# Attention with a routed feed-forward layer on one core: the row maxima of the scores placed by 512 small transfers of single numbers, and another order of work at both ends

## The reference

```python
def _L0_attn_ref(x, w_q, w_k, w_v, w_o):          # x: (4, 1024, 128), 16 heads of 64
    scale = 1.0 / sqrt(64)
    q = einsum('bsd,hdk->bhsk', x, w_q); k = ...; v = ...
    scores = einsum('bhqk,bhmk->bhqm', q, k) * scale
    weights = softmax(scores, axis=-1)
    z = einsum('bhqm,bhmk->bhqk', weights, v)
    z = transpose(z, (0, 2, 1, 3)).reshape(b, s, h * dk)
    return x + einsum('bse,ed->bsd', z, w_o)

def _L0_ffn_ref(x, Wr, W1, W2):                   # 8 experts, 512 rows each at most
    probs = softmax(xf @ Wr); eidx = argmax(probs); p_tok = probs[eidx]
    rank = (number of earlier tokens with the same expert); keep = rank < cap
    xe = xf[dispatch]
    ye = relu(xe @ W1) @ W2 * p_tok               # token's own expert only
    return y.at[dispatch].add(ye)

x = L0_attn_x
x = x + _L0_attn_ref(_layernorm(x), ...)
x = x + _L0_ffn_ref(_layernorm(x), ...)
```

## Time and profile before

| | |
|---|---|
| median of 3 runs | 1506.01 us (1503.90 to 1507.67) |
| the profiled execution's own time | 1504.45 us |
| its span in the profile | 1502.5 us, so 1.95 us lie around it |
| PE, PE's loads | 98%, 56% of the span |
| DVE, ACT, POOL | 66%, 52%, 81% |
| granted TensorE clock, mean | 0.992 |
| DMA packets | 125293, 137.88 MB |

### The profile page before, as it was taken

One profiled execution on the slowest core, in us unless ns is written; L12 is line 12 of the kernel. 1 busy time (PEld: TensorE's weight loads), 2 busy tenths in 40 slices (PEclk: granted clock), 3 DMA queues, 4 the chain that ended last, 5 costly groups with the idle time before them and its releaser, 6 DMA issues.

```text
span 1502.5 us, 21668 instructions
## 1 busy us (share of the span) xinstructions
PE 1477.6 (98%) x7240; PEld 840.9 (56%) x7240; DVE 995.6 (66%) x1222; ACT 784.0 (52%) x1540; POOL 1217.7 (81%) x676
## 2 busy tenths in 40 slices
PE   8999999999999999999999999999999999999897
PEld 5455555555555555555555555555555655555586
DVE  6557666676767656666666666676667766777543
ACT  4465555555555555555555555565554555544331
POOL 5888779898798878988788878889789998899645
PEclk9999999999999999999999999999999999999899
DMA  6334444432444434333344443334444334340431
GB/s 146 84 86 98 92 114 101 115 93 59 93 100 93 115 83 94 86 79 84 86 107 101 97 94 78 85 86 93 95 96 101 89 72 102 92 107 23 133 84 34
DMA packets 125293, 137.88 MB, mean 92 GB/s; under 512 B 44106, under 2 KB 69197, under 8 KB 125184
## 3 DMA queue, kind: packets, MB, share of 16 engines
q1 hardware_dynamic: 118784, 130.26, 37.3%
q0 software_dynamic: 2048, 4.10, 0.9%
q10 hardware_dynamic: 4352, 2.13, 0.5%
HBM read 16.81 MB, written 8.45 MB: 17 GB/s over the span
## 4 chain that ended last, share of the span: by engine, by line
PE 88%; POOL 5%; DVE 3%; issue 1%; ACT 1%; SPq 1%; DMA 1%; POOLq 0%; ACTq 0%; DVEq 0%
PE ps_w L1391 27%; PE ps_w L1375 16%; PE ps_w L1376 14%; PE ps_m L1323 10%; POOL acc L662 4%; PE ps_m L1424 3%; PE ps_w L1409 2%; PE ps_m L1291 2%; PE ps_m L1292 2%; PE ps_m L1293 2%; PE ps_w L1698 1%; PE ps_m L1698 1%; PE ps_m L1308 1%; PE ps_m L1309 1%; PE ps_m L1310 1%
## 5 line engine op out<-in xcount | busy, mean ns | idle before, releaser
L662 POOL TENSOR_TENSOR acc<-acc,ring 128x1024 f32<-128x1024 f32 x383 | 920.8, 2404 | 50.3 <-ACT ring L831 2.3
L1063 DVE TENSOR_REDUCE mxw<-ps_m 128x1 f32<-128x1024 f32 x512 | 601.8, 1217 | 324.1 <-PE ps_m L1323 321.1
L831 ACT ACTIVATE ring<-ps_w 128x512 f32<-128x512 f32 x1024 | 544.3, 600 | 251.6 <-PE ps_w L1376 236.4
L1391 PE MATMUL ps_w<-ring,V 128*64 128x512 f32 x2048 | 467.7, 598 | 0.0
L1375 PE MATMUL ps_w<-queriesA,keysA 128*128 128x512 f32 x1024 | 431.6, 422 | 2.7 <-issue 1.4
L1376 PE MATMUL ps_w<-queriesB,keysB 65*128 65x512 f32 x1024 | 406.4, 397 | 0.0
L1391 PEld LDWEIGHTS ps_w<-ring,V 128*64 128x64 f32 x2048 | 135.7, 136 | 265.5 <-issue 236.1
L662 POOL TENSOR_TENSOR acc<-ring 128x1024 f32<-128x1024 f32 x64 | 152.2, 2377 | 158.9 <-PE ps_w L1409 150.6
L1375 PEld LDWEIGHTS ps_w<-queriesA,keysA 128*128 128x128 f32 x1024 | 193.6, 189 | 103.5 <-issue 48.7
L1376 PEld LDWEIGHTS ps_w<-queriesB,keysB 65*128 65x128 f32 x1024 | 194.4, 190 | 33.6 <-issue 0.7
L1323 PE MATMUL ps_m<-keysA,queriesA 64*128 64x512 f32 x1000 | 183.0, 444 | 0.9 <-DVE mxw L1063 0.6
(11 more groups left out here) (185 smaller groups left out, 985.5 us busy)
## 6 DMA issues: line engine op xcount, KB each, us to landing
queriesA<-qk_high SPq DMA_DIRECT2D x248, 128.0 KB, 2.4
keysB<-qk_high SPq DMA_DIRECT2D x124, 128.0 KB, 2.4
keysA<-qk_rest SPq DMA_DIRECT2D x124, 128.0 KB, 2.4
queriesB<-qk_rest SPq DMA_DIRECT2D x124, 128.0 KB, 2.4
by_sums<-sums SPq DMA_DIRECT2D x240, 64.0 KB, 2.0
keysA<-qk_high SPq DMA_DIRECT2D x93, 128.0 KB, 2.4
tokens_by_slot<-blank ACTq DMA_DIRECT2D x16, 130.0 KB, 3.2
ring<-tokens_by_slot SPq DMA_DIRECT2D x8, 260.0 KB, 5.3
```

The costliest lines, as they stand in the source:

```text
L662: pool.tensor_tensor(acc[h][:, :], before, P_both(kt), ALU.add).then_inc(summed, 1)
L831: act.activation(P_tile(kt, p), ps_s[k % 3][:, :], ACT.Exp, scale=SCALE).then_inc(exp_done, 1)
L1063: dve.tensor_reduce(mxw[h][:, p * HT + qt:p * HT + qt + 1], ps_m[p][:, :], AX_X, ALU.max).then_inc(maxed, 1)
L1391: mm = pe.matmul(ps_z[p * DK:(p + 1) * DK, :], V_of(j, kt, p), P_tile(kt, p), start=(kt == 0), stop=(kt == KT - 1))
```

## The change

Between column and row nothing is computed any more. `turn_max` and `copy_max`, the tiles `mxt` and the semaphores `c_turned` and `c_copied` are gone. `place_max` waits for the last maximum itself (`maxed`) and issues, for each of the two heads and each of the four query tiles, one transfer from a column of `mxw[h]` (128 partitions, one number of 4 B each) to 128 neighbouring numbers of the row: 8 issues in place of 2, 1024 single numbers in place of 8 rows of 512 B. DVE waits for `c_placed`, where it waited for `c_turned`, before it writes over `mxw[h]`. The rest is order at the ends: the first projections of values stand between the first visits, there are 21 turns of `spin` at the start where there were 16, `choose`, `add_totals` and `find_slots` stand ahead of `end_root`, the moments are a part of their own (`end_moments`), PE counts the ranks ahead of the last softmax sums, and ACT copies these sums ahead of `shares`.

```diff
-        mxw = [sb(f"mxw{i}", [P, 2 * HT]) for i in range(2)]
-        mxt = [sb(f"mxt{i}", [2 * HT, P], F32R) for i in range(2)]
+        mxw = [sb(f"mxw{i}", [P, 2 * HT], F32R) for i in range(2)]
...
             def place_max(j, par, h):
-                sp.wait_ge(c_copied, 2 * j + h + 1)
+
+                sp.wait_ge(maxed, 8 * (2 * j + h) + 8)
                 for p in range(2):
-                    sp.dma_start(queriesB[par][p][DK:KC, h * HALF:(h + 1) * HALF].bitcast(F32)
-                                 .rearrange("o (t q) -> o t q", q=P),
-                                 mxt[h][p * HT:(p + 1) * HT, :].bitcast(F32)).then_inc(c_placed, 16)
+                    for t in range(HT):
+                        at = h * HALF + t * P
+                        sp.dma_start(queriesB[par][p][DK:KC, at:at + P].bitcast(F32),
+                                     mxw[h][:, p * HT + t:p * HT + t + 1].bitcast(F32)).then_inc(c_placed, 16)
...
-            def copy_max(j, h, bank):
-                act.wait_ge(c_turned, 2 * j + h + 1)
-                act.activation(mxt[h][:, :], bank[0:2 * HT, 0:P], ACT.Copy).then_inc(c_copied, 1)
...
             copy_z(LAST, 1)
+            copy_sums_out(LAST, 1)
             shares(B - 1)
-            copy_sums_out(LAST, 1)
...
-                            dve.wait_ge(c_turned, 2 * j + (1 if oct == 1 else 2))
+                            dve.wait_ge(c_placed, 128 * (2 * j + (1 if oct == 1 else 2)))
...
             in_order(dve, pair)
+            choose(B - 1, lent_out)
+            add_totals(B - 1)
+            find_slots(B - 1, lent_out)
             end_root(0)
             end_root_done(0)
-            choose(B - 1, lent_out)
             shift(B - 1)
-            add_totals(B - 1)
-            find_slots(B - 1, lent_out)
+            end_half(1)
             find_shares(B - 1)
-            end_half(1)
+            end_moments(1)
...
-            def turn_max(j, h, bank):
-                pe.wait_ge(maxed, 8 * (2 * j + h) + 8)
-                pe.transpose(bank[0:2 * HT, 0:P], mxw[h][:, :], ident[:, :]).then_inc(c_turned, 1)
...
                 if k == 0 and oct % 2 == 0:
-                    pe.wait_ge(c_placed, 32 * (2 * j + h) + 32)
+                    pe.wait_ge(c_placed, 128 * (2 * j + h) + 128)
...
-            spin(16)
+            spin(21)
...
             first_visit(0, 0)
+            pe.wait_ge(first_copied, 1)
+            project_v(0, 0, 0, 0, ps_s[0])
             first_visit(1, 1)
             first_visit(1, 0)
-            pe.wait_ge(first_copied, 1)
-            project_v(0, 0, 0, 0, ps_s[0])
+            pe.wait_ge(first_copied, 2)
+            project_v(0, 0, 1, 0, ps_s[1])
             first_visit(2, 1)
             first_visit(2, 0)
-            pe.wait_ge(first_copied, 2)
-            project_v(0, 0, 1, 0, ps_s[1])
+            pe.wait_ge(first_copied, 3)
+            project_qk(1, 1, 0, 0)
...
+            count_ranks(B - 1, lent_out)
             softmax_sums(LAST, 1, LAST_BY_PE)
-            count_ranks(B - 1, lent_out)
```

More of the change, by code:

```diff
@@ L860, in pair @@
                         cast_qk(1, 1, 2)
-                    if oct == 1:
-                        copy_max(j, 1, lent_max)
-                    if oct == 3 and not last:
-                        copy_max(j + 1, 0, lent_max)
                     if early(j, 0) is not None and oct >= 2:
@@ L1106, in end_half, with end_moments @@
                                                  op0=ALU.mult, op1=ALU.add).then_inc(end_added, 1)
+            def end_moments(h):
+                n, b = 2 * B - 1, B - 1
                 for t in range(h * HT, (h + 1) * HT):
@@ L1557, in pair @@
                         count_ranks(routed(j, "d"), lent_turn)
-                    if oct == 1:
-                        turn_max(j, 1, lent_max)
-                    if not last and oct == 3:
-                        turn_max(j + 1, 0, lent_max)
                     for k in range(5, 8):
@@ L1589, in pair @@
                             pe.wait_ge(ranks_read, routed(j, "d") + 1)
-                        if oct in (1, 3):
-                            pe.wait_ge(c_copied, 2 * j + 2 + oct // 2)
                         if oct == 1:
```

7 lines of the change are left out of this document (1 added, 6 removed).

## The result

| | before | after |
|---|---|---|
| median (4 runs each) | 1504.95 us (1502.17 to 1507.67) | 1692.47 us (1681.08 to 1703.92) |
| ratio to before, 95% interval | | 1.1247 [1.1207, 1.1288] |
| the profiled execution's own time | 1504.45 us | 1691.89 us |
| its span; mean granted clock | 1502.5 us; 0.992 | 1689.9 us; 0.939 |

What follows compares the result with a forecast made beforehand. PE, busy for 98% of the span, was taken to bound the kernel. 1504.45 - 7 (transposition) + 90 (waits) + 48 (clock) - 1 - 1.5 (ends) = 1633 us, range 1550 to 1690 us.

Steps and rivals of the forecast that it cites:

- Eight issues, second half: SP's issues of the second half's maxima, 0.64 us each, make PE wait 2.8 us at oct 2: 32 waits, 90 us.
- The 32nd wait: The very first placement, ahead of pair 0's first scores, counted as one more PE wait of 2.8 us.
- Single numbers: Maxima moved as 4 B numbers: 75 ns a packet, 0.60 us per transfer, keeping pace with issues; landing 2.0 us after issue.
- Rivals 1 and 3: 1: single numbers issue quickly, PE doesn't wait, 1495 us, 5%; 3: single numbers are slow, some 1890 us, 8%.
- Eight issues for two, first half of the next pair: Maxima land 2.3 us before PE wants them; SP's 0.9 us delay is absorbed waiting for use 3's cast; cost nothing.
- The clock: After PE's waits in 28 of 31 pairs, 3.42 us at half speed, 1.7 us lost each: 48 us, bounds 0 to 96.
- The transposition: PE's 64 transpositions of the maxima go, 0.11 us each: 7 us off PE.
- The ends: New order at start and end of the kernel: 1 us and 1.5 us less, bounds 0 to 4 us.
- The range: 1550 to 1690 us for the whole kernel's time, with 17% outside.
- upper bound for the clock: Half-clock stretches after PE's waits twice as long as the 3.42 us taken: 96 us in place of 48.

## Why the prediction was wrong

**Eight issues, second half: right.** 0.64 us each, landing 2.0 us after the last, a wait of 2.83 us in pair 16 where 2.8 was worked out, 31 such waits at the start of oct 2. The distance from before is +89.3 us in oct 1, against 83.3. In the typical pair oct 1 grew by 2.8 us where 2.7 were counted. Seven pairs grew by 3.4 to 4.0 us, and in six of them a single issue, among the eight or just ahead of them, took 1.2 to 1.9 us; eight grew by 2.1 to 2.4. That the sum over all comes out so near is in part luck. The 32nd wait, at the start, was to bring the first tile 1.8 us later (2.8 less 1 from the visits). It came 1.5 us later, but PE waited only 0.65 us: much of the work just ahead of the tile ran at half clock. The Trainium skill's sentence that the time to initiate a DMA is usually small beside the DMA itself ("DMA: Bandwidth & Descriptors", section on issuing engines that are not separate DMA queues) does not carry over to these: one issue is a third of the 2.0 us to its landing, and for eight in a row the issues add up while the landings overlap, 5.1 us of issue and 2.0 us of landing.

**Single numbers: right.** 1024 packets of 4 B took 9 ns each and never set the pace; the 2.0 us to the landing was right. Rivals 1 and 3 are out: the form of the transfer cost no less to issue, and only 0.3 us more to land than a row of 512 B (1.7 us, in the kernel with eight issues of rows), some 10 us over the 31 waits.

**"Eight issues for two, first half of the next pair. Cost nothing": wrong, and the largest part of the miss (30 of 59 us).** That PE doesn't wait for these maxima was right: they landed 0.3 to 2.2 us ahead in pairs 1 to 31. Two things in the step were not. It put SP at the weights 0.9 us later. SP came to L404 at 817.06 with pair 16's start at 819.64, 2.6 us ahead where it was 4.6 us ahead: 2.0 us later, since the eight took 6.02 us and not 5.1 (one of them 1.6 us). In pair 9 they took 6.26 us and use 0 was 3.1 us later. And the step held that the delay is taken up in the wait for use 3. That is true of use 3, but uses 0 and 1 come first, and ACT rewrites their buffers in oct 0. The timeline of ACT beside SP's would have shown it: before, use 0's last issue at 419.37 landed some 2.0 us later, at 421.4, and the cast came at 422.50. That is 1.1 us to spare, against a delay of 2 to 3 us. The step was priced by the last consumer behind the queue and not by the first.

**The clock: the kind right, the size off (71 us in oct 2, forecast 48).** The clock fell behind 27 of 31 waits; 28 were assumed. In the 29 pairs without logits oct 2 grew by 49.7 us, near the forecast's 48, and that is in part luck: 24 stretches of 3.4 to 6.8 us, 4.8 us on the mean, in place of 28 of 3.42. The term was mis-sized by three pairs: 21.3 us in pairs 24, 26 and 28, where the work behind the wait holds the small matmuls of the logits. The stretch of 13.6 us at 0.50 in the earlier trace rows holds matmuls of the same kind (L1445 at the end of the kernel before), but also waits of up to 1.4 us, so it could have given a bound for these pairs and no more. The repeat of the changed kernel lost only 3 us in these three pairs. Why the clock stayed up behind four waits of 2.2 to 2.9 us (pairs 7, 21, 22 and 27) and fell behind the others is open.

**The transposition: right**, 0.11 us in each place, as forecast, seen where nothing covers it. **The ends: wrong by 2.5 us**, they gave nothing. At the start of the profiled execution of after, the second head's part of the fifth visit is 1.2 us earlier than before (24.99 for 26.18 us), but the clock falls to half at 26.0, during the spin behind it, for 10.2 us; before, it stood at full there.

**The range** ended at 1690, and the median of 1692 lies just over it. Its upper bound for the clock (twice the stretch in each of 28 pairs) would have covered oct 2; it was never added to a loss in oct 0, which had no bound at all since the step stood at nothing.

## What to carry to other kernels

Count issues, not bytes: on this kernel each further transfer from one place in SBUF to another took 0.64 us on SP's queue, whether it carried 64 rows of 2 KB, one row of 512 B or 128 single numbers, and whoever adds six of them has to follow each instruction behind them to the first engine that waits for its landing, buffer reuse included. If the added issues can stand in a wait that the queue has anyway, they are free: 1692 us became 1502 us by order alone. And price a new wait of PE with what comes behind it: the wait itself was 90 us, its clock another 70.

## What was not expected of the hardware

- A single wait of PE of 1.6 us was enough for the clock to fall for 3.4 us (twice, with runs of two numbers), and one of 2.9 us could leave it up (pairs 21 and 22).
- Loading weights of 64x128 with every fourth number of SBUF took 317 ns, every second 192 ns, neighbours 184 ns.
- A transfer of 128 single numbers of 4 B between places in SBUF landed 2.0 us after its issue, as one of 128 rows of 32 B from HBM did, and a single row of 512 B after 1.7 us; its packets took 9 ns each.
- Matmuls with 8 columns behind a wait kept the granted clock at half for 13.7 to 20.5 us in 15 of 24 cases; in the other nine it came back after 3.4 to 6.8 us, as without them, or did not fall. In one case the clock fell behind such matmuls for 6.8 us though PE had not waited at all.
